# Embedding front in four groups with the mix on TensorE, parameter loads behind the row gathers, and three small reorderings behind the scan

## The chip, the cores and the metric

The kernel runs on one core of a Trainium2 chip. The core has five engines that run their own instruction lists side by side: TensorE (PE; its weight loads are PEld), VectorE (DVE), ScalarE (ACT), GpSimd (POOL) and SyncE (SP, used here to issue DMAs). They wait for each other on semaphores only. The metric is the device time of one execution in microseconds (us); the figure for a kernel is the median of its runs.

## What is computed

One layer of a small language model over 8 sequences of 256 tokens, 192 channels wide. Cut to what matters here:

```python
# embedding: 64 values of the token's row, and two mixes of 3 rows each
emb = emb_table[tokens]                                   # (8, 256, 64)
parts = [emb]
for i, spos in enumerate((spos0, spos1)):                 # spos: (3, 64)
    sel = softmax(emb[..., 3*i:3*(i+1)], axis=-1)
    parts.append(einsum('bsk,kd->bsd', sel, spos))
h = concatenate(parts, axis=-1) * sqrt(192) + positional_encoding(256, 192)

# selective-scan layer
n = layernorm(layernorm(h))                               # second with gamma, beta
xi, z = split(n @ W_in, 2)                                # 384 channels each
u = silu(depthwise_conv1d(xi))                            # 3 taps along the sequence
y = merge of a forward and a backward selective scan of u
h = h + (layernorm(y) * silu(z)) @ W_out + layernorm(h)

# mixture of experts, top 2 of 8
h = h + sum over the two experts picked by a router of gate * expert(layernorm(h))
```

## The kernel before, in words

**Tiles.** A tile (`t`) is 128 tokens on the 128 partitions; there are 16 (`TILES`). A group (`g`) is 4 tiles, 512 tokens, two sequences; there are 4 (`NG`). The 384 inner channels are 3 blocks (`blk`) of 128.

**Front, to about 88 us.** POOL gathers the token rows with 16 indirect DMAs, one per tile (L561), and only then builds `ident`, the unit matrix that every transpose on PE needs. Everything up to the second norm is done in two halves of 8 tiles (`HT`): `select` (L689 to L698) makes the softmax of the two triples with small DVE operations and one exponential on ACT (L1117); `mix_in` (L700) multiplies and adds the three `spos` rows over 8 tiles at a time, five DVE operations of 512 columns for each mix; of the second half, POOL does the second mix (L583, L586). `embed` (L711) scales, adds the position table and takes the moments; `norm_twice` (L719) applies both norms, with the roots from ACT (L1109, L1110) and one Newton step on DVE. The order on DVE is: the whole first half, `select(1)` and `mix_in(1, 0)`, `embed(1)`, `norm_twice(1)`, and only then `convolve(0)`. ACT scales the rows by the second root (`norm_in`, L1137, L1139), PE transposes them (`norm_transposes`), ACT applies gamma and beta (`keep_xn_t`, L1149), and PE multiplies with W_in (`in_products`, L1471 and L1474), two banks at a time for groups 2 and 3. DVE convolves from the banks (L776 to L780), ACT keeps z (L1160) and u (L1164). `keep_lb(0)` (L1171) opens the next stage, the time steps.

All 34 small parameter loads are on SP's queue in one list (L466) under one semaphore `s_par`. DVE, POOL, ACT and PE each wait for the whole list before the work that follows in their own lists.

**Scan, 140 to 614 us.** 192 turns, in each of which DVE scans, POOL multiplies, ACT makes decays and scaled inputs, and PE transposes. The change does not touch it.

**Behind the scan.** ACT issues the load of `w_out` after the last sum of PE (L1325). PE waits for it and for the last copy of y out of the banks (`s_yv`, written by DVE at L856) before `y_transposes(0)`. The router follows. Then DVE works out for each of the 39 slots of 128 rows (`SLOTS`) which rows it holds: `is_slot` (L1021, 32 x 39 = 1248 columns), its product with `row_hi` and with `row_lo` into `hot_a` (L1023, twice), the places `hot_b` in four parts (L1027), and PE multiplies the two (L1715) behind its `b2` products (L1709). From the result come `src_row` and `dst_row`.

**Slots, 694 to 880 us.** POOL gathers the 128 rows of a slot (L629), six or seven slots ahead; at first two gathers are issued and both are waited for (L634) before ACT hears of either. ACT copies the slot's rows (L1401) and weights (L1417), PE transposes (L1451), ACT keeps the transpose (L1409), PE multiplies (L1738, L1743, L1755), DVE squares the rectified sums, and POOL scatters the result.

## Time and profile before

| | us |
|---|---|
| median of 3 runs | 904.82 |
| lowest and highest run | 903.65 and 904.99 |
| the profiled execution, device time | 903.25 |
| its span, first to last instruction | 901.5 |

The device time of the profiled execution is 1.75 us more than its span. Busy shares over the whole span are PE 86%, PEld 78%, DVE 81%, ACT 72% and POOL 59%; the chain that ended last is PE for 47%, DVE for 22% and ACT for 17% of the span. These are means over stages with different limits, so the stages are read by themselves: the first 88 us, the 39 us behind the scan, the 41 us of routing, and the slots. In the rows, "idle before" is how long the engine stood still ahead of a group and the name behind the arrow is what ended that; PEclk is the granted TensorE clock as a share of 2.4 GHz.

### The profile page before, as it was taken

To read this page: it belongs to the slowest core of one execution; us is meant where nothing else is said; L and a number is where in the kernel's file an instruction comes from. 1 tells how busy PE (TensorE), PEld (TensorE's weight loads), DVE (VectorE), ACT (ScalarE), POOL (GpSimd) and SP (SyncE) were. 2 spreads that over 40 slices of the span, in tenths; PEclk is the share of its full clock that TensorE was granted. 3 is DMA by queue.
4 is the path that set the end of the run, shared out by engine and by line. 5 is a ranking of instruction groups with operands and counts; after the bars stand their busy time and mean duration, and the time that the engine had idled before them with its cause. 6 is when DMAs were issued, how large, how long until landed. Compare 5 with 4: busy or idle time off the path is not lost.

```text
span 901.5 us, 16654 instructions
## 1 busy us (share of the span) xinstructions
PE 778.9 (86%) x6060; PEld 706.4 (78%) x6061; DVE 730.8 (81%) x871; ACT 648.5 (72%) x1261; POOL 535.1 (59%) x343
## 2 busy tenths in 40 slices
PE   0389777899999999989999899996956999999990
PEld 0133336899998999989999899995855899999990
DVE  3788899789999899988999999998938455555554
ACT  0365999999999999989999999992331444444421
POOL 6430004799988999969999799892000444444420
PEclk9999988999999999999999999997955899999996
DMA  4003103355674754745746466376450111111106
GB/s 87 3 30 111 9 27 123 89 137 175 148 212 149 165 191 123 195 140 130 210 113 163 159 180 187 118 167 230 136 171 9 40 44 44 44 44 44 44 23 218
DMA packets 46453, 104.43 MB, mean 116 GB/s; under 512 B 16448, under 2 KB 25176, under 8 KB 46392
## 3 DMA queue, kind: packets, MB, share of 16 engines
q1 hardware_dynamic: 35784, 74.67, 25.6%
q0 software_dynamic: 8352, 27.07, 15.1%
q10 hardware_dynamic: 2256, 1.87, 0.6%
q8 instruction: 38, 0.62, 0.3%
q14 instruction: 23, 0.19, 0.1%
HBM read 83.77 MB, written 19.82 MB: 115 GB/s over the span
## 4 chain that ended last, share of the span: by engine, by line
PE 47%; DVE 22%; ACT 17%; POOL 7%; issue 4%; DMA 2%; DVEq 0%; ACTq 0%; POOLq 0%; SPq 0%
PE ps L1451 15%; PE ps L1755 8%; PE ps L1573 8%; DVE arena L851 8%; ACT arena L1278 6%; PE ps L1738 6%; POOL arena L625 5%; ACT arena L1261 4%; PE ps L1743 4%; ACT arena L1264 3%; PE ps L1471 2%; PE ps L1474 1%; DVE stats L672 1%; DVE arena L798 1%; PE ps L1673 1%
## 5 line engine op out<-in xcount | busy, mean ns | idle before, releaser
L625 POOL TENSOR_TENSOR arena<-arena 128x1024 f32<-128x1024 f32 x192 | 395.3, 2285 | 117.3 <-DVE arena L851 114.0
L851 DVE TENSOR_TENSOR_SCAN arena<-arena,ps 128x1024 f32<-128x1024 f32 x192 | 426.3, 2277 | 20.1 <-PE ps L1573 16.9
L1451 PE MATMUL ps<-ident,arena 128*128 128x128 f32 (+3 forms) x2622 | 349.3, 280 | 79.2 <-ACT arena L1139 37.7
L1451 PEld LDWEIGHTS ps<-ident,arena 128*128 128x128 f32 (+3 forms) x2622 | 299.7, 144 | 100.6 <-issue 52.0
L1278 ACT ACTIVATE arena<-arena,neg_a 128x510 f32<-128x510 f32 x384 | 241.0, 708 | 0.1
L629 POOL DMA_INDIRECT arena<-x_rows,arena x39 | 37.8, 970 | 160.2 <-DVE arena L1035 79.6
L1573 PE MATMUL ps<-arena,ln_in 128*128 128x128 f32 x768 | 104.0, 279 | 0.0
L1573 PE MATMUL ps<-arena 128*128 128x128 f32 x768 | 101.4, 275 | 0.0
L1573 PEld LDWEIGHTS ps<-arena,ln_in 128*128 128x128 f32 x768 | 96.0, 196 | 0.0
L1573 PEld LDWEIGHTS ps<-arena 128*128 128x128 f32 x768 | 93.3, 192 | 0.0
L1755 PE MATMUL ps<-arena,ln_in 128*128 x468 | 82.7, 327 | 0.8 <-DVE arena L1066 0.8
L1264 ACT ACTIVATE arena<-ident,arena 128x128 f32<-128x128 f32 x256 | 81.0, 388 | 0.0
L1755 PEld LDWEIGHTS ps<-arena,ln_in 128*128 128x128 f32 x468 | 75.1, 190 | 1.2 <-issue 1.1
L1261 ACT ACTIVATE arena<-ln_in,arena 128x384 f32<-128x384 f32 x128 | 68.1, 605 | 3.1 <-PE ps L1573 2.7
L1261 ACT ACTIVATE arena<-arena 128x384 f32<-128x384 f32 x128 | 67.9, 602 | 2.6 <-PE ps L1573 2.5
L637 POOL DMA_INDIRECT y_rows<-arena x39 | 38.5, 988 | 30.9 <-DVE arena L1066 19.1
L1409 ACT ACTIVATE arena<-ps 128x256 f32<-128x256 f32 x39 | 15.0, 384 | 56.2 <-PE ps L1451 56.2
L1053 DVE TENSOR_TENSOR ln_in<-ps,arena 128x384 f32<-128x384 f32 x40 | 22.1, 554 | 40.1 <-PE ps L1743 40.1
L1053 DVE TENSOR_TENSOR ln_in<-ps,ln_in 128x384 f32<-128x384 f32 x38 | 21.0, 553 | 34.3 <-PE ps L1743 34.3
L1417 ACT ACTIVATE arena<-arena 128x1158 f32 x20 | 23.4, 1170 | 33.4 <-issue 14.2
L1061 DVE SCALAR_TENSOR_TENSOR ln_in<-ln_in 128x384 f32<-128x384 f32 x78 | 43.5, 558 | 2.7
L1417 ACT ACTIVATE ln_in<-arena 128x1158 f32 x19 | 22.2, 1170 | 20.9 <-issue 17.4
(218 smaller groups left out, 882.5 us busy)
## 6 DMA issues: line engine op xcount, KB each, us to landing
arena<-b_rows SPq DMA_DIRECT2D x64, 512.0 KB, 4.0
arena<-ws SPq DMA_DIRECT2D x16, 576.0 KB, 6.3
arena<-wf POOLq DMA_DIRECT2D x16, 576.0 KB, 8.2
arena<-hf POOLq DMA_DIRECT2D x16, 576.0 KB, 7.9
summed_first<-arena SPq DMA_DIRECT2D x8, 576.0 KB, 5.4
summed_second<-arena SPq DMA_DIRECT2D x8, 576.0 KB, 7.3
arena<-summed_second SPq DMA_DIRECT2D x8, 576.0 KB, 5.8
gates_dram<-arena SPq DMA_DIRECT2D x4, 768.0 KB, 3.4
```

The costliest lines, as they stand in the source:

```text
L625: g_.tensor_tensor(state[i % STATES], state[i % STATES], c_bc[u % C_BUFS], ALU.mult).then_inc(s_mul, 1)
L851: v.tensor_tensor_scan(o, a, x, 0.0, ALU.mult, ALU.add).then_inc(s_scan, 1)
L1053: added = v.tensor_tensor(hid, ps[:, H_BANKS[half] + i, 0:HH].rearrange("p (a b) -> p a b", b=P), bias[:, 3 * i:3 * (i + 1)].unsqueeze(2). ...
L1061: v.scalar_tensor_tensor(hid, hid, 0.0, hid, ALU.max, ALU.mult).then_inc(s_h[i], 1)
L1261: a.activation(x_t[u % 2][:, t, :], dtu_t[g % 2][d][:, t, :], ACT.Copy, scale=bt[:, TG * g + t, col:col + 1])
L1264: last = a.activation(b_diag[u % 2][:, t, :], ident[:], ACT.Copy, scale=bt[:, TG * g + t, col:col + 1])
L1278: last = a.activation(out_a[:, n, :, lo:hi], src[:, :, lo:hi], ACT.Exp, scale=neg_a[:, blk, d, PAIR * pair + n:PAIR * pair + n + 1])
L1417: a.activation(w1_cur[half], w1_all[:, bass.ds(e * WC, WC)], ACT.Copy).then_inc(s_wc, 1)
L1451: return mm(o, src, ident[at:at + parts, at:at + parts], start=start, stop=True, is_transpose=True, skip_group_check=True)
L1573: last = mm(ps[:, bank + 1, P * t:P * t + P], dtu_t[g % 2][d][:, t, cols], b_diag[u % 2][:, t, :], start=True, stop=True)
L1738: mm(ps[:, H_BANKS[half] + j // 3, P * (j % 3):P * (j % 3) + P], w1_cur[half][:, P * j:P * j + P], slot_x_t[half][:, 0, :], start=j % 3 == ...
L1755: last = mm(ps[:, 3, 0:C], h_t[half][:, j, :], w2_all[:, bass.ds(e * (HB * C) + j * C, C)], start=j == 0, stop=j == HB - 1)
```

## The change

Front:

- POOL builds `ident` ahead of the gathers. The gathers count on four semaphores, one for each group.
- The select, the position sum and both norms go group by group, in an order written out by hand on DVE, ACT and PE in which the steps of several groups alternate.
- The mix becomes a product on PE: the six weights of each of a group's four tiles (24 columns) are transposed, ACT keeps the transpose, and one product of 24 rows with a block-diagonal `mix_w` (24 x 512, filled by eight small DMAs on ACT's queue) gives the 128 mixed values of all four tiles in one bank. DVE reads them from the bank.
- The position table is loaded twice over, so that it covers four tiles.
- SP's list is cut: the first 9 loads (channel constants, W_in, gamma and beta) count on `s_win`; the other 25 are issued once all rows have been gathered. The waits for `s_par` move behind the work that doesn't need it.
- The exponential of the decay rates and the waits for parameters move to later places; POOL's sum of residual and norm waits for groups instead of halves.

Behind the scan:

- PE's waits for `w_out` and for the router weights move from ahead of `y_transposes(0)` into the products that read them.
- `row_lo` depends on the partition only, so its product with `is_slot` becomes two ACT copies with a per-partition scale; PE waits for these too. `row_hi` is made directly.
- Slot 0 is gathered alone and ACT hears of it at once; then pairs (1, 2), (3, 4), (5, 6). ACT does `keep_x_t(0, 0)` before `copy_x(1, 1)`.

```diff
-            pool.wait_ge(s_tok, 16)   # ... 16 gathers, then ident
+            st.then(g_.memset(ident[:], 0.0))
+            g_.affine_select(out=ident[:], in_=ident[:], compare_op=ALU.not_equal, fill=1.0, base=0,
+                             pattern=[[-1, P]], channel_multiplier=1).then_inc(s_ident, 1)
+            pool.wait_ge(s_tok, 16)   # ... 16 gathers, .then_inc(s_rows[t // TG], 16)
...
-            for dst, src in loads:
+            for dst, src in loads[:WIN_LOADS]:
+                sp.dma_start(dst, src, allow_slow_non_contiguous=True).then_inc(s_win, 16)
+            for g in range(NG):
+                sp.wait_ge(s_rows[g], 16 * TG)
+            for dst, src in loads[WIN_LOADS:]:
                 sp.dma_start(dst, src, allow_slow_non_contiguous=True).then_inc(s_par, 16)
...
+            act.wait_ge(s_mix_z, 1)
+            for t in range(TG):
+                for i in range(2):
+                    row = SEL * t + NPOS * i
+                    act.dma_start(mix_w[row:row + NPOS, t, SUB * i:SUB * (i + 1)],
+                                  spos[:, NPOS * SUB * i:NPOS * SUB * (i + 1)].rearrange("o (k c) -> (o k) c", k=NPOS)).then_inc(s_mix_w, 16)
...
+            def select_transpose(g):
+                pe.wait_ge(s_sel_w, g + 1)
+                transpose(ps[0:TG * SEL, SEL_BANK, P * g:P * (g + 1)], sel_w[:, TG * g:TG * (g + 1)].rearrange("p t i k -> p (t i k)"), P).then_inc(s_sel_ps, 1)
+            def mix_product(g):
+                if g == 0:
+                    pe.wait_ge(s_mix_w, 16 * 2 * TG)
+                pe.wait_ge(s_sel_t, g + 1)
+                if g == 3:
+                    pe.wait_ge(s_emb, 1)
+                mm(ps[:, MIX_BANKS[g], :], sel_t[g % 2], mix_w.rearrange("p t c -> p (t c)"), start=True, stop=True).then_inc(s_mix_ps, 1)
...
# DVE, front order
-            select(0); mix_in(0, 0); mix_in(0, 1); embed(0); norm_twice(0)
-            select(1); mix_in(1, 0); embed(1); norm_twice(1)
+            select_logits(0); embed_rows(0); select(0); embed_mix(0)
+            select_logits(1); embed_rows(1); norm_first(0); select(1); norm_rows(0); norm_second(0)
+            select_logits(2); embed_rows(2); select(2); embed_mix(1)
+            select_logits(3); embed_rows(3); norm_first(1); select(3); norm_rows(1); norm_second(1)
+            embed_mix(2); embed_mix(3); norm_first(2); norm_rows(2); norm_second(2)
+            norm_first(3); norm_rows(3); norm_second(3)
+            dve.wait_ge(s_win, 16 * WIN_LOADS)
...
# ACT, front order
+            select_exp(0); keep_sel_t(0); first_root(0); select_exp(1); second_root(0); keep_sel_t(1); norm_in(0)
+            select_exp(2); keep_sel_t(2); act.wait_ge(s_win, 16 * WIN_LOADS); keep_xn_t(0)
+            first_root(1); select_exp(3); second_root(1); keep_sel_t(3); norm_in(1)
+            first_root(2); first_root(3); second_root(2); keep_xn_t(1); norm_in(2); second_root(3)
+            # then neg_a, and keep_z(0, blk)
...
# PE, front order
+            select_transpose(0); mix_product(0); select_transpose(1); mix_product(1)
             norm_transposes(0)
+            select_transpose(2); mix_product(2); pe.wait_ge(s_win, 16 * WIN_LOADS)
             pe.wait_ge(s_xn_t, 2)
             in_products(0, (0, 1))
+            select_transpose(3); mix_product(3)
             in_products(0, (2,))
             norm_transposes(1)
+            pe.wait_ge(s_emb, 3)
             in_products(0, (3, 4))
+            pe.wait_ge(s_emb, 4)
             in_products(0, (5,))
...
             pe.wait_ge(s_yv, NG)
-            pe.wait_ge(s_w_out, 16)
-            pe.wait_ge(s_wr, 1)
             def out_product(g):
+                pe.wait_ge(s_w_out, 16)
...
-            for h, part in enumerate((row_hi, row_lo)):
-                st(v.tensor_tensor(hot_a[:, :, h, :], is_slot, each(part[:], SLOTS), ALU.mult))
+            v.tensor_tensor(hot_a[:, :, 0, :], is_slot, each(row_hi[:], SLOTS), ALU.mult).then_inc(s_hot_a, 1)
+            # on ACT:
+            for k in range(TOP):
+                rows_k = slice(TILES * k, TILES * (k + 1))
+                a.activation(hot_a[:, rows_k, 1, :], is_slot[:, rows_k, :], ACT.Copy, scale=row_lo[:, k:k + 1]).then_inc(s_hot_a, 1)
...
-            for s in range(0, AHEAD, 2):
+            gather(0)
+            gathered(1, 1)
+            for s in range(1, AHEAD, 2):
                 gather(s)
                 gather(s + 1)
                 gathered(s + 2, 2)
-            gather(AHEAD)
```

## Rows read from the trace of the kernel before

**Rows 1.** Engine busy times by stage: routing, and slots; PEclk, DMA share, GB/s last.
```profile
653.00:694.00 41.00, 29.08 (x148) 26.14 (x148) 25.55 (x120) 9.44 (x17) 0.00 (x0) 0.54 0.30 100
705.00:876.00 171.00, 170.78 (x1436) 161.63 (x1437) 94.77 (x190) 71.92 (x147) 69.42 (x71) 1.00 0.15 42
```

**Rows 2.** Timeline of POOL, front: start, us, engine, line, operation, idle before.
```profile
2.80 1.10 POOL L561 DMA_INDIRECT arena<-emb,tok_sb  x1 [2.28 <-DMA tok_sb<-tok]
...
20.91 1.15 POOL L561 DMA_INDIRECT arena<-emb,tok_sb  x1 [0.30 <-issue]
22.37 1.14 POOL L561 DMA_INDIRECT arena<-emb,tok_sb  x1 [0.30 <-issue]
...
23.96 1.40 POOL L566 TENSOR_SCALAR_AFFINE_SELECT ident<-ident 128x128 f32<-128x128 f32 x1 [0.23 <-issue]
```

**Rows 3.** POOL's DMA queue: packets, MB, share, in 2 to 9.5 and 2 to 25 us.
```profile
q0 software_dynamic: 128, 0.13, 8.6%
...
q0 software_dynamic: 512, 0.53, 12.0%
```

**Rows 4.** Timeline of DVE, front.
```profile
15.96 0.21 DVE L696 TENSOR_TENSOR arena<-arena 128x48 f32<-128x48 f32 x1
16.20 0.69 DVE L706 TENSOR_TENSOR ln_in<-arena 128x512 f32<-128x512 f32 x1
...
23.45 1.76 DVE L715 SCALAR_TENSOR_TENSOR resid<-ln_in,arena 128x1536 f32<-128x1536 f32 x1
25.25 2.18 DVE L672 BATCH_NORM_STATS2 stats<-resid 128x6 f32<-128x192 f32 x8
...
29.81 2.40 DVE L729 TENSOR_SCALAR ln_in<-resid,mv,rs 128x192 f32<-128x192 f32 x8
...
38.53 1.43 DVE L706 TENSOR_TENSOR arena<-arena 128x512 f32<-128x512 f32 x1
```

**Rows 5.** Timeline of ACT, front.
```profile
33.10 1.49 ACT L1137 ACTIVATE arena<-ln_in,rs 128x192 f32<-128x192 f32 x4 [2.47 <-DVEq L734]
...
88.18 0.76 ACT L1171 ACTIVATE arena<-ps,row_one,row_scale 128x512 f32<-128x512 f32 x1
```

**Rows 6.** Timeline of PE, front.
```profile
35.19 1.94 PE L1451 MATMUL ps<-ident,arena 128*128 128x128 f32 x8 [35.19 <-ACT arena L1139]
38.92 3.38 PE L1471 MATMUL ps<-arena 128*128 128x512 f32 x4 [1.79 <-ACT arena L1149]
...
58.94 1.97 PE L1451 MATMUL ps<-ident,arena 128*128 128x128 f32 x8 [2.47 <-ACT arena L1139]
...
67.39 1.88 PE L1471 MATMUL ps<-arena 128*128 128x512 f32 x4
```

**Rows 7.** Timeline of SP's queue, front: the last of the 34 loads.
```profile
20.52 0.72 SPq L466 DMA_DIRECT2D b_sb<-b  x1
```

**Rows 8.** Timeline behind the scan, DVE and PE.
```profile
616.81 1.75 DVE L856 COPY arena<-ps 128x1536 f32<-128x1536 f32 x1
...
620.63 2.79 PE L1451 MATMUL ps<-ident,arena 128*128 128x128 f32 x12 [4.93 <-DMA arena<-w_out]
```

**Rows 9.** Timeline of the slot tables, PE and DVE.
```profile
681.21 8.44 PE L1709 MATMUL ps<-b_sb,ln_in 8*128 8x192 f32 x32 [0.68 <-ACT ln_in L1392]
...
685.99 1.45 DVE L1023 TENSOR_TENSOR arena<-arena,row_lo 128x1248 bf16<-128x1248 f32 x1
...
692.16 0.70 PE L1715 MATMUL ps<-arena 128*128 128x78 bf16 x8 [0.44 <-DVE arena L1027]
```

**Rows 10.** Timeline of the first slots, POOL, ACT, PE.
```profile
694.14 1.09 POOL L629 DMA_INDIRECT arena<-x_rows,arena  x1 [79.59 <-DVE arena L1035]
...
698.24 0.36 ACT L1401 ACTIVATE arena<-arena 128x192 f32<-128x192 f32 x1 [1.90 <-POOLq L634]
...
698.95 0.94 POOL L629 DMA_INDIRECT arena<-x_rows,arena  x1 [2.44 <-DMA arena<-x_rows,arena]
...
705.22 1.57 PE L1738 MATMUL ps<-arena,ln_in 128*128 128x128 f32 x12 [0.52 <-issue]
```

More of the change, by code:

```diff
@@ L213, in build @@
         sel_r = cut([TILES, 2])
-        mix = [cut([HT, SUB]) for _ in range(2)]
+        mix_w = cut([TG, 2 * SUB], parts=TG * SEL)
+        sel_t = [cut([P], parts=TG * SEL) for _ in range(2)]
         used[0] = after_params
@@ L396, in build @@
         s_place = sem("places_ready")
+        s_is_slot = sem("slot_flags_ready")
+        s_hot_a = sem("row_parts_ready")
         s_held = sem("held_product")
@@ L650, in _ @@
                 pool.wait_ge(s_y, s + 2)
+                if s and s + AHEAD - 1 < SLOTS:
+                    gathered(s + AHEAD, 1)
                 if s + AHEAD < SLOTS:
-                    gathered(s + AHEAD + 1, 1)
-                if s + AHEAD + 1 < SLOTS:
-                    gather(s + AHEAD + 1)
+                    gather(s + AHEAD)
                 scatter(s)
@@ L661, in _ @@
             st = Steps(dve, v_step)
+            v.memset(mix_w, 0.0).then_inc(s_mix_z, 1)
             v.memset(w_x, 0.0)
@@ L700, in mix_in @@
-            def mix_in(h, i):
-                half = slice(HT * h, HT * (h + 1))
-                dst = ln_in[:, half, SUB * (i + 1):SUB * (i + 2)]
-                for k in range(NPOS):
-                    o = dst if k == 0 else mix[0]
-                    st.then(v.tensor_tensor(o, spos_sb[:, i:i + 1, k, :].to_broadcast([P, HT, SUB]),
-                                            sel_w[:, half, i, k:k + 1].to_broadcast([P, HT, SUB]), ALU.mult))
-                    if k:
-                        st.then(v.tensor_tensor(dst, dst, mix[0], ALU.add))
@@ L721, in norm_twice, with of_group @@
-            def norm_twice(h):
-                half = slice(HT * h, HT * (h + 1))
-                dve.wait_ge(s_rstd, h + 1)
-                newton(HT * h, HT, mv, rs)
-                st.then(v.tensor_tensor(nt1[:, half], rs[:, half], rs[:, half], ALU.mult))
-                v.tensor_tensor(mv2[:, half, 1], mv[:, half, 1], nt1[:, half], ALU.mult).then_inc(s_ln_in, 1)
-                for t in range(HT * h, HT * (h + 1)):
+            def of_group(g):
+                return slice(TG * g, TG * (g + 1))
@@ new lines, in embed_mix, with norm_first @@
+            def embed_mix(g):
+                dve.wait_ge(s_mix_ps, g + 1)
+                embedded(g, slice(SUB, C), ps[:, MIX_BANKS[g], :].rearrange("p (t c) -> p t c", t=TG)).then_inc(s_emb, 1)
+                dve.wait_ge(s_emb, g + 1)
+                st.wait()
+                moments(lambda t: resid[:, TG * g + t, :], TG * g, TG, mv, s_ln)
+            def norm_first(g):
+                group = of_group(g)
+                dve.wait_ge(s_rstd, g + 1)
+                newton(TG * g, TG, mv, rs)
+                st.then(v.tensor_tensor(nt1[:, group], rs[:, group], rs[:, group], ALU.mult))
+                v.tensor_tensor(mv2[:, group, 1], mv[:, group, 1], nt1[:, group], ALU.mult).then_inc(s_ln_in, 1)
@@ L781, in convolve @@
                                            cv[:, :, 0:SEQ - 1], ALU.mult, ALU.add).then_inc(s_conv, 1)
-            norm_twice(1)
+            select_logits(0)
+            embed_rows(0)
+            select(0)
+            embed_mix(0)
+            select_logits(1)
+            embed_rows(1)
+            norm_first(0)
+            select(1)
+            norm_rows(0)
+            norm_second(0)
+            select_logits(2)
+            embed_rows(2)
+            select(2)
+            embed_mix(1)
+            select_logits(3)
+            embed_rows(3)
+            norm_first(1)
+            select(3)
+            norm_rows(1)
+            norm_second(1)
+            embed_mix(2)
+            embed_mix(3)
+            norm_first(2)
+            norm_rows(2)
+            norm_second(2)
+            norm_first(3)
+            norm_rows(3)
+            norm_second(3)
+            dve.wait_ge(s_win, 16 * WIN_LOADS)
             convolve(0)
             convolve(1)
+            dve.wait_ge(s_par, 16 * PAR_LOADS)
             constants()
```

196 lines of the change are left out of this document (99 added, 97 removed).

## Prediction

> **What bounds the kernel now.** I read the stages first, since the busy shares of the whole are a mean over them. The slots run at PE's own pace: PE is busy 170.78 of 171 us at the full clock [rows 1], and the change leaves the 39 slots' work alone. The scan is 192 equal turns that the change leaves alone too. So what can move is the start of the scan, the stretch between scan and slots, and the first slot. Then the timelines of one engine after another, front first, with the question who ends each engine's idle time.
>
> In the front, PE has its first work at 35.19 us and its first product with W_in at 38.92 [rows 6]. Before that it is a chain of DVE: the first eight tiles are gathered, DVE mixes them with ten operations of 512 columns at 0.69 us [rows 4], scales and adds (1.76), takes moments, norms, and ACT gets the first rows at 33.10 [rows 5]. PE then works on group 0 and 1 and stands still again for 2.47 us until the second half has been normed (58.94, [rows 6]). From 67.39 it runs six pairs of blocks without a gap, and the stage ends where ACT opens the time steps, 88.18 [rows 5]. The front is bound by its serial chain, not by any engine's work: the lever is when the first rows reach PE, and that each later group is ready when PE asks.
>
> Behind the scan PE stands still 4.93 us, and what ends it is the load of w_out [rows 8]. In the routing DVE makes tables while PE waits, at a mean granted clock of 0.54 [rows 1]; the first slot waits until 698.24 for two gathers, though it needs one [rows 10].
>
> **The front, step by step.** The new order has three engines handing work around, so I lay it out from the rows and carry one clock time along. Handoffs cost 0.05 us each.
>
> *Rows arrive.* POOL's queue has moved 128 packets of its 512 by 9.5 us, a quarter, so the first four gathers have landed by then; all 512 by 25 [rows 3]. `ident` first costs POOL nothing: memset and select (1.40) fit into the 2.28 us for which it waits for the tokens [rows 2]. What hides it is that load; without it, it would cost some 1.9. I take 9.6, 14.6, 19.7 and 25.2 for the groups. ACT's eight small loads are issued long before 9.6 (ACT has nothing else until then); they land in time unless each took over 1 us.
>
> *Group 0 to PE.* Two select operations on DVE 0.4 and rows to place 0.35 (256 of the 1536 columns of the 1.76 us operation, plus start), exponential on ACT hidden behind the latter, three small operations 0.6 (0.21 each, [rows 4]): weights at 11.0. PE transposes 24 columns. No row shows this shape; the nearest are eight full transposes in 1.94 [rows 6], so 0.25 to 0.7, taken 0.45. ACT's copy 0.3. The product of 24 rows with 512 columns: a full 128-row one takes 3.38 / 2 = 1.7 on the same slow clock and about half that later [rows 6]; the depth is smaller but not the columns, so I take 1.75 (0.85 to 2.5). DVE reads the bank 0.8, moments 1.5 (half of 2.18 plus aggregation): 16.0. DVE then does the logits and rows of group 1 (0.75), six operations of 0.2 for the first norm (as the 0.21 of [rows 4]), the weights of group 1 (0.6), four rows of norm at 0.30 (2.40 / 8), four operations more (0.83): 20.6. The root on ACT (two small operations, 0.5) hides behind group 1's work. ACT's `norm_in(0)` is one half of what it did, 1.9: 22.6. It began at 33.10; now at 20.65.
>
> *First product.* PE transposes 1.94: 24.6; then, ahead of the product in PE's list, the weights of group 2 (0.45), ACT's copy 0.3 and the 1.38 for gamma and beta, the mix product 1.75 beside it: W_in starts at 27.2 instead of 38.92. That is **11.7 us**.
>
> *Holding it.* PE: first pair 4.4, then group 3's weights, copy and mix 2.6, third block 2.1, transposes 1.0, pair 2.8, last block 2.1: 42.2. Group 3's rows (25.2) are asked for at 25.8, so there is 0.6 us of slack. Next late is ACT's copy of z behind `norm_in(2)` and the last root: ACT is busy from 39.8, hands over at 43.6, so PE stands still 1.4. From there PE's list has no gap: 3.0 + 2.1 + 1.0 + 2.8 + 2.1 + 1.0 reaches group 2's products at 55.7, before at 67.4 [rows 6]. DVE's convolutions begin at 43.1, behind the last norm, at 2.3 a block, and keep ahead of PE by 0 to 2 us. Six pairs follow, and the stage ends at 76.4 instead of 88.18: **11.8 us**.
>
> *What else moves.* The 25 late loads: SP issued its 34 from 2.4 to 20.52 + 0.72 = 21.24 [rows 7], 0.55 us apiece, so 25 of them take from 25 to 39, landed by 42. First reader is the projection at 73 on PE and the constants on DVE at 59, so 17 us of cover; SP's next duty, storing the gates, comes at about 54. POOL's sums start at 44 and are wanted after 90. The second mix leaves POOL; beside it DVE's multiplications had taken 1.43 instead of 0.69 [rows 4], and that cost is gone too (it is in the 11.8).
>
> The Trainium skill ("SBUF — State Buffer", section "Who interferes with whom") says that a DVE operation with two SBUF inputs and a GpSimd one that reads SBUF block each other; the 1.43 beside 0.69 agrees. The same section speaks against the new order: single-input DVE operations in a two-port mode keep GpSimd from writing the descriptors of its gathers. The norm rows and copies now run while gathers are issued. What the rows show of that: the last two gathers start 1.46 us apart, once DVE's wide operations run; if the last four have that pitch, the first eleven steps had (20.91 - 3 x 1.45 - 2.80) / 11 = 1.25 [rows 2]. At 1.45 for the eight others too the last group lands 1.6 later, 1.0 more than its slack: at most 1 us of the 11.8.
>
> **Behind the scan.** `y_transposes(0)` still needs the banks free: DVE's copy ends at 616.81 + 1.75 = 618.56 [rows 8]. So it starts at 618.6, not 620.63: **2.0 us**, all of it passed on, since ACT and DVE stand idle for its result. w_out is next read by `out_product(0)` some 8 us later and has landed by 620.6. Between 1 and 2.
>
> **Slot tables.** DVE loses one operation of 1.45 [rows 9]; ACT, idle, does two halves in about 0.7 each, beside DVE's product with `row_hi`. The parts of `hot_b` come 1.45 earlier, but PE is in its b2 products until 681.21 + 8.44 = 689.65 [rows 9] and then has 32 products of some 0.07: 691.85 instead of 692.86. **1.0 us** (0.5 to 1.45).
>
> **First slots.** The gather of slot 0 starts at 694.14 and alone should land in 2.7; ACT can copy at 696.9, not 698.24, and PE gets the first product 1.3 earlier. But gather 1 is now issued only behind it, after the 0.7 us that POOL takes from landing to the next gather (ACT hears at 698.24, POOL starts the next at 698.95, [rows 10]), and slots 1 and 2 land at 701.5. ACT's copies then queue: x of slot 1, its weights (1.17), x of slot 2, and the second slot's products start at 704.35 instead of 705.22 [rows 10]. **0.9 us** (0 to 1.4). Also 3.41 us of DVE sums gate the first transpose at 697.5, no later than the new order asks.
>
> **Sum:** 11.8 + 2.0 + 1.0 + 0.9 = 15.7. Span 901.5 - 15.7 = 885.8, device time of the profiled execution 903.25 - 15.7 = 887.6; against the median of 904.8 it gives 889.1. The forecast is 888.5, between the two.
>
> **Rivals.** *The front gives less.* Three handoffs (DVE, PE, ACT, PE, DVE) take the place of DVE's private mix. At 0.1 a handoff it is 0.9 dearer, with products at 2.5 another 2.2, with late gathers 1: the front gives 8 and the time is 892.3. For it: PE at the start is at half clock. Against: slack in DVE's own list.
>
> *The front gives more.* If PE has the full clock by its first products, mixes cost 0.85 and the layout ends 1.6 earlier; if the routing, shifted against the clock's changes, gets the full clock for some of its 41 us (now 0.54, [rows 1]), 2 to 3 more: 884.5.
>
> *The tail pieces don't do what they say.* The waits for the y copy, for DVE's last sums and for slot 1's gather take the place of those removed; 2 us go: 890.5. For it: each of the three has a second wait within 2 us.
>
> *Slower.* The scan is not changed but is entered with its engines in another phase. DVE's scan and POOL's product run side by side there, and [rows 4] show what DVE can lose beside a reading POOL (1.43 for 0.69). If the new phase makes the two overlap more, so that each of the 192 turns is 0.1 us longer, 19.2 us are lost against 15.7 won and it is 908. It decides from (15.7 + 1.8) / 192 = 0.09 us a turn on. Against: everything that feeds the first turn shifts together, and turns are long compared with the handoffs.
>
> **How the numbers follow.** As laid out 0.60; front gives less 0.20; front gives more 0.12; tail pieces void 0.05; slower scan 0.03. The range 884.0 to 893.5 takes in the first four with their bounds. About 0.2%, 1.8 us, is what a measurement of this kernel can tell from no change; within it would need the front to give nothing, which no row supports: 0.01, taken out of the second case. Faster 0.96, slower 0.03.
>
> **What would show it.** ACT's first scaling of rows at 20 to 22 us; first W_in product at 26 to 29; no PE gap over 2 us from there; the opening of the time steps at 75 to 79; the first transpose behind the scan waiting for DVE's copy and not for w_out; PE's last table product within 0.3 of the end of its b2 products plus 2.3; PE busy all through the slots as before. Wrong would be a W_in product after 31, a row group landing after 27, or a scan whose 192 turns take over 2 us longer in all.

## The result, and the profile after

The changed kernel takes 889.45 us (888.67 to 890.06, 4 runs) against 904.24 (903.4 to 904.99) for the kernel before on the same chip: a ratio of 0.9836, 95% interval 0.9819 to 0.9853. The forecast was 888.5 in 884.0 to 893.5. The profiled execution after has 889.05 us and a span of 887.3, against 903.25 and 901.5.

In words, the stages of both profiled executions, each from one event to the next:

| stretch | before | after | gain |
|---|---|---|---|
| start to ACT's opening of the time steps | 88.18 | 76.30 | 11.88 |
| to DVE's first turn of the scan | 56.09 | 56.97 | -0.88 |
| to DVE's last copy of y | 472.54 | 473.39 | -0.85 |
| to PE's `b2` products | 64.40 | 61.86 | 2.54 |
| to POOL's first slot gather | 12.93 | 11.81 | 1.12 |
| to PE's second slot of products | 11.08 | 10.41 | 0.67 |
| to the end | 196.28 | 196.56 | -0.28 |
| span | 901.5 | 887.3 | 14.2 |

So two stretches that the change does not touch, the time steps and the scan, give back 1.73 us of what was won, and the slots another 0.28. That is the part that the prediction did not have, and many of the experiments below are about it.

The front first. Timeline of the kernel after, POOL, DVE, ACT and PE (start, us, engine, line, operation, idle before and what ended it); the rows answer to [rows 2, 4 to 6]:

```profile
1.25 0.28 POOL L571 TENSOR_SCALAR_AFFINE_SELECT ident<-ident 128x128 f32<-128x128 f32 x1 [0.24 <-POOL ident L570]
2.77 1.12 POOL L575 DMA_INDIRECT arena<-emb,tok_sb  x1 [1.24 <-DMA tok_sb<-tok]
...
20.43 0.94 POOL L575 DMA_INDIRECT arena<-emb,tok_sb  x1 [0.30 <-issue]
21.68 0.94 POOL L575 DMA_INDIRECT arena<-emb,tok_sb  x1 [0.30 <-issue]
...
10.47 0.18 DVE L695 TENSOR_REDUCE arena<-arena 128x8 f32<-128x24 f32 x1 [7.62 <-DMA arena<-emb,tok_sb]
...
14.95 0.69 DVE L689 SCALAR_TENSOR_TENSOR resid<-ps,arena 128x512 f32<-128x512 f32 x1 [3.04 <-PE ps L1513]
...
21.66 1.49 ACT L1163 ACTIVATE arena<-ln_in,rs 128x192 f32<-128x192 f32 x4 [1.39 <-DVEq L735]
...
12.06 0.37 PE L1497 MATMUL ps<-ident,arena 128*24 128x128 f32 x1 [12.06 <-DVE arena L708]
12.88 2.04 PE L1513 MATMUL ps<-arena 24*128 24x512 f32 x2 [0.45 <-ACT arena L1147]
...
28.19 3.78 PE L1530 MATMUL ps<-arena 128*128 128x512 f32 x4
...
43.62 1.96 PE L1530 MATMUL ps<-arena 128*128 128x512 f32 x4 [0.55 <-ACT arena L1180]
...
55.51 1.88 PE L1530 MATMUL ps<-arena 128*128 128x512 f32 x4
```

To see: PE's first work is a transpose at 12.06, not at 35.19; W_in's first product comes at 28.19, not at 38.92; and the only idle time of PE from there on is 0.55 us. The unit matrix took 0.28 us at 1.25, where before it took 1.40 at 23.96, beside DVE's two-input operation that ran from 23.45 to 25.21 [rows 2, 4]; behind the first (1.12) every gather takes 0.94 or 0.95, and from the second on each starts 1.25 behind the one before it, to the end, where the last ones had taken 1.15 and 1.14.

Behind the scan, timeline of PE, DVE, ACT and POOL after; they answer to [rows 8 to 10]:

```profile
608.46 1.93 PE L1497 MATMUL ps<-ident,arena 128*128 128x128 f32 x12 [2.92 <-DVE arena L874]
...
671.85 1.52 ACT L1439 ACTIVATE arena<-arena,row_lo 128x624 bf16<-128x624 f32 x2 [3.38 <-DVE arena L1039]
...
676.80 2.26 PE L1785 MATMUL ps<-arena 128*128 128x78 bf16 x32
...
680.33 1.10 POOL L625 DMA_INDIRECT arena<-x_rows,arena  x1 [75.93 <-DVE arena L1052]
...
683.34 0.36 ACT L1447 ACTIVATE arena<-arena 128x192 f32<-128x192 f32 x1 [0.51 <-POOLq L630]
...
688.07 0.36 ACT L1447 ACTIVATE arena<-arena 128x192 f32<-128x192 f32 x1 [3.06 <-POOLq L630]
```

The first transpose behind the scan now waits for DVE's copy and no longer for w_out; the 32 table products run in one piece straight behind the `b2` products; ACT copies slot 0's rows 3.01 us after the gather is issued, where it had taken 4.10 (698.24 - 694.14).

What was lost lies in the granted clock (1.00 is the level of 2.4 GHz, 0.50 that of 1.2 GHz). The first two rows are windows of the kernel before, in the time steps and behind the start of a scan group (the scan goes through the four groups one after another); the next three are windows of the kernel after, over a product in the time steps and behind two such starts. Columns: window, length, busy time of PE, PEld, DVE, ACT, POOL, then PEclk, DMA share, GB/s:

```profile
108.00:116.00 8.00, 5.52 (x10) 2.57 (x11) 7.86 (x6) 7.33 (x10) 0.00 (x0) 0.79 0.03 8
...
276.40:286.20 9.80, 9.80 (x91) 9.74 (x91) 9.49 (x5) 9.50 (x21) 8.98 (x6) 1.00 0.29 112
```

```profile
98.60:104.06 5.46, 5.46 (x7) 2.36 (x8) 5.36 (x4) 3.71 (x4) 0.00 (x0) 0.50 0.01 3
...
265.00:275.00 10.00, 10.00 (x79) 10.00 (x78) 8.79 (x5) 8.56 (x18) 8.00 (x5) 0.84 0.38 126
...
500.40:510.00 9.60, 9.60 (x75) 9.60 (x74) 8.50 (x5) 7.75 (x16) 7.62 (x5) 0.83 0.30 100
```

At each start of a scan group PE is idle for over a third of some 9.7 us, and behind that the clock either stays at 1.00 (before, 276 us: 91 products in 9.80 us) or falls for a while (after, 265 us: 79 in 10.00, 0.84). Such a fall is called a dip below. From one of DVE's copies of y to the next there were 117.11, 118.72 and 114.34 us before, and 118.72, 117.10 and 115.77 after: a dip costs 1.4 to 1.6 us. Before has one at these three starts, after has two; with the stretch ahead of the first start 0.57 shorter (121.80 for 122.37) that is the 0.85.

### The profile page after: what moved, and what is told of

It is laid out like the page before. It is cut to its first block, busy times and chain, and to the rows that moved or that the text cites. A ratio compares the mean times of both kernels' runs of the same rounds, so it can differ in the third digit from the quotient of the medians.

```text
span 887.3 us, 16729 instructions
## 1 busy us (share of the span) xinstructions
PE 786.0 (89%) x6072; PEld 707.1 (80%) x6073; DVE 721.1 (81%) x890; ACT 651.6 (73%) x1275; POOL 525.6 (59%) x339
## 4 chain that ended last, share of the span: by engine, by line
PE 51%; DVE 20%; ACT 17%; POOL 5%; issue 4%; DMA 2%; ACTq 0%; DVEq 0%; POOLq 0%; SPq 0%
PE ps L1497 16%; DVE arena L869 9%; PE ps L1825 8%; PE ps L1643 8%; ACT arena L1319 6%; PE ps L1808 6%; ACT arena L1302 4%; POOL arena L621 4%; PE ps L1813 4%; ACT arena L1305 2%; PE ps L1530 2%; PE ps L1533 1%; PE ps L1742 1%; DVE stats L670 1%; ACT arena L1327 1%
```

## Experiments

The kernels ran in three groups, with the kernel before beside each, at 905.48, 905.14 and 904.86 us. Stages are read in each one's profiled execution.

### One half of the change alone

`front_only` is the changed kernel with the work behind the scan as before (the `row_lo` product in two halves on DVE); `tail_only` the kernel before with the three pieces behind the scan. The core of the edit that tells them apart:

```diff
# front_only, from the changed kernel
+            pe.wait_ge(s_w_out, 16)
+            pe.wait_ge(s_wr, 1)
             def y_transposes(g):
...
+            for k in range(TOP):   # row_lo part on DVE again
...
-AHEAD = 7
+AHEAD = 6
```

> The front of the changed kernel with the parts behind the scan as before. Theory (the pieces add): the time steps open at 76.3 us as in the changed kernel, not 88.2, and some 1.7 us of the 11.9 are given back between there and the end of the scan, as in the changed kernel, because TensorE's granted clock rises at other moments after its idle gaps; nothing is won behind the scan. Time 10.2 us under the kernel before, 894.0. Rival A (the 1.7 us are given back by something that the new front leaves behind, such as the late parameter loads on SP's queue): same time here, but then the kernel whose parameter loads are early gets them back. Rival B (the pieces behind the scan depend on the new front): more than 14 us are missing from the sum of this kernel and the one with the tail alone.

> The kernel before with only the parts behind the scan changed: w_out wait moved, low row part on ScalarE, slot 0 gathered alone with AHEAD 7. Theory: time steps open at 88.2, and from there to the end of the scan it takes 528.6 us as before; then 2.0 us at the w_out wait, 0.5 in the routing, 1.1 at the row parts and 0.7 at the first slots: 4.3 us under the kernel before, 899.9. Rival (the tail pieces are covered by second waits and what was seen came from shifted clock phases): within 1.5 us of the kernel before, 902.7 or more.

`front_only` took 892.53 us, ratio 0.9866 (0.9848 to 0.9884): 12.1 us for the front. `tail_only` took 901.36, ratio 0.9958 (0.9941 to 0.9974): 3.8 us for the three pieces, where 3.9 was forecast. These gains are worked out from the ratios; the medians lie 12.95 and 4.12 apart. Together 15.9 against the 14.8 measured for both; each gain is known to about 1.6 us only, which leaves room for a plain sum. The rival that the tail pieces win under 1.5 us is out (the interval is 2.3 to 5.3). `front_only` did better than its forecast of 10.2: its time steps open at 75.08 and not at 76.3, and only the scan gave something back. In `tail_only` the time steps took 56.10 and the scan 472.63, in `front_only` 56.08 and 473.23.

### Where the front's gain sits: the unit matrix, and the place of the mix

`ident_late` builds the unit matrix behind the 16 gathers again. `mix_dve` keeps the four groups, the early unit matrix and the new orders, and does the mix with DVE operations of 256 columns.

```diff
# ident_late
-            st.then(g_.memset(ident[:], 0.0))
-            g_.affine_select(out=ident[:], in_=ident[:], ...).then_inc(s_ident, 1)
             pool.wait_ge(s_tok, 16)   # ... 16 gathers
+            st.then(g_.memset(ident[:], 0.0))
+            g_.affine_select(out=ident[:], in_=ident[:], ...).then_inc(s_ident, 1)
# mix_dve, DVE
-                dve.wait_ge(s_mix_ps, g + 1)
-                embedded(g, slice(SUB, C), ps[:, MIX_BANKS[g], :].rearrange("p (t c) -> p t c", t=TG)).then_inc(s_emb, 1)
+                for i in range(2):
+                    for k in range(NPOS):
+                        o = mix_t if k else dst
+                        st.then(v.tensor_tensor(o, spos_sb[...], sel_w[...], ALU.mult))
+                        if k:
+                            st.then(v.tensor_tensor(dst, dst, mix_t, ALU.add))
+                embedded(g, slice(SUB, C), mixed).then_inc(s_emb, 1)
```

> The changed kernel with the unit matrix built behind the 16 gathers, as in the kernel before. It is ready at about 23.2 us. Theory (the mix on TensorE hangs on it, and the front's chain has no slack from there): the first transpose of weights starts at 23.3 instead of 12.1, the first product with W_in at 39 to 40 instead of 28.2, the time steps open at 87 to 89, so the whole gain of the front is gone: 900 to 901. Rival (only the first group is late, and since all rows are in by then the later groups catch up): the time steps open at 79 to 82 and the time is 892 to 895.

> The changed kernel with the mix done by VectorE in four groups (ten operations of 256 columns a group, position rows loaded by broadcast as before) and no transposes of weights or mix products; all else, the order of the groups too, as changed. Theory (the mix on TensorE is what pays: DVE is the front's next bound): ten operations of 0.39 us replace a handoff of 3.0 us, so group 0 is 1 us later at ACT (about 22.6), the first W_in product is at 28 as in the changed kernel, but DVE has 15.6 us more work with under 6 us of idle time to put it in, so the convolutions start some 10 us later (54 instead of 43.9), and the time steps open at 86 to 88. Time 899 to 901. Rival (the split into groups is what pays, since it lets PE begin early): the time steps open at 77 to 80 and the time is 890 to 893.

`ident_late` took 901.82 us, ratio 0.9948 (0.9931 to 0.9965): as `tail_only`, so the front's gain is gone. Its time steps open at 87.22, against 88.18 before. Timeline of its PE:

```profile
23.37 0.39 PE L1497 MATMUL ps<-ident,arena 128*24 128x128 f32 x1 [23.37 <-POOL ident L576]
24.20 2.04 PE L1513 MATMUL ps<-arena 24*128 24x512 f32 x2 [0.45 <-ACT arena L1147]
```

The transpose of the weights waits for `ident` until 23.37, 11.31 us later than after, and W_in's first product is at 39.43, 11.24 later. Once the mix is on PE, the unit matrix is the head of the front's chain; before, PE had no use for it until 35.19.

`mix_dve` took 908.24 us, ratio 1.0037 (1.0022 to 1.0051): slower than before, though it has all of the front but the mix on PE, and all of the tail. Its first W_in product comes early (31.84), but the time steps open at 95.60. Groups of instructions of its DVE, 9 to 95 us (line, operation, operands, count, busy us and mean ns, idle before), and its window from the first W_in product to the opening:

```profile
L719 DVE TENSOR_TENSOR arena<-arena 128x256 f32<-128x256 f32 x24 | 10.2, 426 | 0.9 <-DVE rs L683 0.2
L775 DVE TENSOR_SCALAR arena<-ps,chan_sb 128x512 f32<-128x512 f32 x12 | 9.7, 804 | 5.8 <-PE ps L1512 5.6 <-DVE rs L683 0.2
...
L722 DVE TENSOR_TENSOR arena<-arena 128x256 f32<-128x256 f32 x16 | 6.8, 425 | 0.5
```

```profile
31.84:95.60 63.76, 52.99 (x129) 18.64 (x129) 53.82 (x145) 29.52 (x65) 6.83 (x2) 0.84 0.14 49
```

The mix is 40 operations and 17.0 us of DVE, which also has to convolve before PE's banks come free. PE is busy 52.99 of 63.76 us there, at a granted clock of 0.84; in the kernel after it is busy 47.21 of 48.11, at 1.00. PE's four stops in this window (3.25, 1.67, 1.95 and 3.89 us) are ended by DVE or by ACT, which had itself waited 15.3 us for DVE's moments; the stage lost these stops and the longer products at the lower clock. The opening was forecast at 86 to 88, so the loss is right in kind and some 8 us larger than thought. The other kernels of its group, with the mix on PE, opened at 79.97 to 80.38. So four groups without the move to PE don't pay in this order of operations, which was written for a mix on PE; an order made for DVE was not tried.

### Whether the late loads cost the time steps

`par_early` issues the 25 late loads at once, with no wait for the rows.

```diff
-            for g in range(NG):
-                sp.wait_ge(s_rows[g], 16 * TG)
             for dst, src in loads[WIN_LOADS:]:
```

> The changed kernel, but SP issues the 25 late parameter loads right behind the 9 early ones, without waiting for the row gathers. Theory (the loads are small and in nobody's way): gathers keep their pitch of 1.25 us, DVE's first operation on rows starts within 0.5 us of the 10.47 of the changed kernel, the time steps open at 76.3 within 0.5, and the time is that of the changed kernel, 889.5 within 1.0. Rival A (their thousands of 4-byte packets hold up the gathers): DVE's first operation at 12 or later and each group 1 to 3 us later, time 891 to 893. Rival B (late loads cost something after the front): time steps plus scan are back at 528.6 instead of 530.4 us, time 887.7.

It took 889.27 us, ratio 0.9825 (0.9799 to 0.9851), no different from the changed kernel within some 2.4 us. W_in at 28.24, time steps open at 75.67; these steps took 56.09 and its scan 473.44. So the cut of SP's list neither buys nor costs anything that can be measured, and it isn't what lengthens the scan.

### The pieces behind the scan, one by one

```diff
# wout_wait_back
             pe.wait_ge(s_yv, NG)
+            pe.wait_ge(s_w_out, 16)
+            pe.wait_ge(s_wr, 1)
# rowlo_dve: DVE again, 2 operations of 624 columns
-                a.activation(hot_a[:, rows_k, 1, :], is_slot[:, rows_k, :], ACT.Copy, scale=row_lo[:, k:k + 1]).then_inc(s_hot_a, 1)
+                v.tensor_tensor(hot_a[:, rows_k, 1, :], is_slot[:, rows_k, :], row_lo[...], ALU.mult).then_inc(s_hot_a, 1)
# weights_first
-            copy_x(1, 1)
             copy_w(1, 1)
+            copy_x(1, 1)
```

> The changed kernel with PE's waits for w_out and the router weights back ahead of the first transposes behind the scan. Theory: the gap of TensorE there grows from 2.9 to 4.9 us and is ended by the DMA; 2.0 us are lost down to the first slot: 891.4. Rival (ACT's and DVE's own work sets the start of the second transposes anyway): under 0.7 us lost, 890.1 or less.

> The changed kernel with the low row part made on VectorE by two products of 624 columns in place of ACT's two copies. Theory: DVE takes 1.5 us more ahead of the places, but TensorE is busy with the b2 products for 0.4 of that, so the last table product ends 1.1 us later: 890.5. Rival (the end of the b2 products sets it alone): no difference, 889.5.

> The changed kernel, but ACT copies the second slot's weights before it waits for that slot's rows. In the changed kernel ACT stands idle 3.06 us for those rows, then copies rows and weights (1.17 us), and TensorE waits 1.45 us for it. Theory (ACT's order is what ate part of the gain of gathering slot 0 alone): the wait shrinks to 0.3 to 0.6 us and the time is 1.0 us less: 888.5. Rival (the gather of slots 1 and 2 itself sets the second slot): under 0.3 us.

The totals (896.32, 893.79 and 894.94 us; ratios 0.9898, 0.9877 and 0.9884) can't be set against 889.45: all kernels of this group had a front that was 4 us later, of which below. Their stages can.

*The wait for w_out.* From DVE's last copy of y to the `b2` products: 63.91 us with the wait put back, 61.77 to 62.01 in the six other kernels of the first two groups that have the new order. The price is 2.0 us, so its rival (under 0.7) is out. Timeline of `wout_wait_back`, PE:

```profile
613.19 1.09 PE L1497 MATMUL ps<-ident,arena 128*128 128x128 f32 x4 [4.87 <-DMA arena<-w_out]
```

*The row parts.* From the end of the `b2` products to the first slot gather: 4.49 us before (12.93 - 8.44), 4.45 in `rowlo_dve` (12.64 - 8.19), 3.47 in the changed kernel. The two ACT copies are worth 1.0 us. But in `front_only`, which has the parts on DVE as well, it is 3.47 too (14.07 - 10.60): there the `b2` products took 10.60 us instead of the 8.2 to 8.9 of most kernels, and DVE was done behind them. This window of `wout_wait_back`, which had the same 10.60, shows why:

```profile
673.33:683.93 10.60, 10.60 (x34) 10.16 (x35) 8.93 (x15) 1.52 (x2) 0.00 (x0) 0.50 0.00 0
```

At 0.50 from end to end, 32 products take 10.60; after has 8.34 at 0.64.

*Weights ahead of rows.* The second slot's products start 5.61 us behind the first, as in most others. That says little on the order of ACT's copies: PE ran this slot at the lower clock, its twelve products took 2.90 instead of the 1.57 of the kernel after, and it had no wait for ACT in front of the second slot ([0.52 <-issue], 694.87). Inconclusive.

### The same kernel again, and the clock filled by hand

`after_again` is the changed kernel, unaltered. `clock_steps` puts 26 transposes of the unit matrix into a free bank in PE's 3.29 us of idle time in the time steps; `clock_slots` puts 10 behind the table products, ahead of slot 0; `clock_all` has both, and the early loads.

```diff
# clock_steps
+                            if g == 2 and d == 0 and blk == 0:
+                                for _ in range(26):
+                                    transpose(ps[:, 0, 0:P], ident[:], P)
                             pe.wait_ge(s_pl, 2 * (g - 1) + d + 1)
# clock_slots
             last.then_inc(s_held, 1)
+            pe.wait_ge(s_passed, 2)
+            for _ in range(10):
+                transpose(ps[:, 0, 0:P], ident[:], P)
             pe.wait_ge(s_acc, 1)
```

> The changed kernel once more, on the chip that also runs the next three kernels. In the group of experiments before this one all kernels with the new front had the W_in product at 31.8 to 32.8 us, where the changed kernel had it at 28.19; the 4 us lay between VectorE's small norm operations in the first norm of group 0, with no semaphore behind them. If this comes from the chip or the execution, the three kernels of this group and this one show the same W_in time, all near 28.2 or all near 32.4. If it comes from the kernel's code, this one is at 28.2 whatever the chip. Time 889.5 (887 to 892) with the early front, 893.5 (892 to 896) with the late one; ratio to the kernel before 0.9836 or 0.988. Time-steps stage 56.08 or 56.97, nothing between.

> The changed kernel with 26 transposes of the identity into a free PSUM bank in the 3.29 us in which TensorE is idle in the time-steps stage. Theory (the 0.88 us that this stage lost is TensorE's clock after the gap, not the late loads): the product behind the gap takes 4.3 us or less instead of 5.46, the stage from the opening to the scan's first turn takes 56.1 or less, in this run and whenever it is profiled, and the total falls by 0.9 against a run of the changed kernel whose stage was 56.97, and by 0 against one whose stage was 56.08. Rival (the late loads or bank order cost it): the stage stays at 56.97. Second rival (the dummy work itself delays the product by running into its start): stage 57.5 or more.

> The changed kernel with 10 transposes of the identity into a free PSUM bank after the last table product, in the 4.84 us in which TensorE waits for the first gathered rows. Theory (slots 0 and 1 run at half the clock because TensorE idled before them: first slot to second 5.59 us against 4.53 later): first product to second slot's product 4.6 to 5.0 us and the first slot's product 2.6 us at most, total 1.0 to 2.0 us below the changed kernel of the same chip. Rival A (the clock falls all the same, the dummies stop too early or are too few): 5.6 us and the total as the changed kernel, within 0.5. Rival B (the first slots are held by the weight conversion of ScalarE, not by TensorE): product times fall but the second slot starts no earlier, total within 0.5.

> Both of the clock edits, and the parameter loads no longer held behind the row gathers. If the gains add: 0.9 from the time steps where the changed kernel's stage was 56.97, 1 to 2 from the slots, and 0 to 0.3 from the loads, so 886.5 to 888 with the early front (W_in at 28.2), 890.5 to 892 with the late one. If the loads, issued at once, take bandwidth from the gathers, the W_in product comes over 0.5 us later than in the other kernels of this chip; a single look has it at 28.24 against 28.19, so no such cost is expected.

Measured: 894.15, 891.76, 892.89 and 896.59 us; ratios 0.9881 (0.9864 to 0.9899), 0.9882 (0.9856 to 0.9908), 0.9875 (0.9857 to 0.9892) and 0.9903 (0.9884 to 0.9922).

*The unaltered kernel* has time steps of 56.09 us and a scan of 472.66, the values of before (56.09, 472.54), and one dip among its three group starts (117.10, 118.73, 114.35). So the new code does not force either loss. Over all 14 profiles the steps take 56.08 to 56.10 or 56.97 to 56.98 and nothing between. Four of the twelve kernels with a new front have the long value (the changed kernel, `ident_late`, `mix_dve`, `weights_first`), and neither of the two with the old one (the kernel before and `tail_only`). The scan takes 472.3 to 472.7 in these two, in `after_again` and in `clock_all`, and 473.2 to 474.1 in the other ten. Whether the new front makes the long values likelier is not shown; two profiles of the old one are too few to tell.

*The steps.* The product behind the 3.29 us gap, in the kernel before, in the kernel after, in `after_again` and in `clock_steps` with the gap filled (timeline of PE):

```profile
110.48 4.29 PE L1543 MATMUL ps<-arena 128*128 128x512 f32 x6 [3.29 <-DVE arena L807]
```

```profile
98.60 5.46 PE L1613 MATMUL ps<-arena 128*128 128x512 f32 x6 [3.29 <-DVE arena L825]
```

```profile
101.53 4.34 PE L1613 MATMUL ps<-arena 128*128 128x512 f32 x6 [3.29 <-DVE arena L825]
```

```profile
98.88 3.06 PE L1497 MATMUL ps<-ident 128*128 128x128 f32 x26
102.00 2.84 PE L1616 MATMUL ps<-arena 128*128 128x512 f32 x6
```

The granted clock over the last three is 0.50, 0.65 and 1.00, and their stage 56.97, 56.09 and 56.09. Over the 14 profiles it goes together without exception: where this product takes 5.45 or 5.46 the stage is long (four), where it takes 2.81 to 4.51 it is short (ten). So the clock behind the gap is the cause of the 0.88, as the expectation had it. `clock_steps` alone would not show it, since three kernels with the gap left open have 2.81 as well. The edit buys nothing where the stage is short already. That another engine sets the stage there fits DVE's load (busy 48.29 of 49.97 us from 83.30 on in the kernel after), but was not tested. Its ratio, equal to that of `after_again`, says the same.

*The slots.* In `clock_slots` slot 0's products took 1.58 us at a granted clock of 1.00, in all other kernels 2.90. But `clock_all` has the same ten transposes in the same place, and stayed at 0.50 (timelines of PE, `clock_slots` and then `clock_all`):

```profile
687.24 1.58 PE L1813 MATMUL ps<-arena 128*128 128x128 f32 x12 [0.56 <-ACT arena L1457]
```

```profile
690.80 2.90 PE L1814 MATMUL ps<-arena 128*128 128x128 f32 x12 [0.56 <-ACT arena L1455]
```

So the filling raised the clock in one profile of two. Where it did, the second slot started 5.49 behind the first instead of 5.62: the faster products did not bring the second slot forward, and its rival B, ACT's work, fits what the timeline of ACT in `clock_slots` shows:

```profile
690.05 0.36 ACT L1449 ACTIVATE arena<-arena 128x192 f32<-128x192 f32 x1 [2.96 <-POOLq L630]
...
690.79 1.17 ACT L1465 ACTIVATE ln_in<-arena 128x1158 f32 x1 [0.23 <-issue]
...
691.87 0.35 ACT L1449 ACTIVATE arena<-arena 128x192 f32<-128x192 f32 x1
...
692.26 0.36 ACT L1457 ACTIVATE arena<-ps 128x256 f32<-128x256 f32 x1
```

ACT hears of slot 1's rows at 690.05, which is the landing of the gather, and copies these rows, slot 1's weights (1.17 us) and the rows of slot 2 before it keeps the transpose that PE waits for. PE stands still 0.93 and 1.67 us meanwhile, falls back in its clock (0.81 over its next twelve products) and takes 6.15 us for the next slot, as in `after_again` (6.18), where the kernel after took 4.60. The filling won at slot 0 what it could not keep at slot 1.

*No version beats the changed kernel.* `clock_all` has the shortest scan of all (472.30) and is last of its group: its W_in product is at 33.56, its `b2` products took 10.60 and its first two slots 12.32 us, where after has 10.19. It was forecast at 890.5 to 892 for a late front, so that forecast failed. The test that it set for the early loads, W_in over 0.5 us later than in the others of its group, came out positive (33.56 against 30.40 to 32.23). The gathers were hardly held up, though: behind the first all but one kept their pitch of 1.25 us and DVE's first operation on rows came at 10.20; what came late is DVE, of which next.

### A front that is 2 to 5 us later in two of three groups

Where the unit matrix is made early, W_in's product came at 27.7 to 28.2 us in the first measurement and the first group. In the second and third group it came at 30.4 to 33.6, in all eight kernels, the unaltered one (30.4) among them. Timeline of DVE after, and of `clock_steps`, in the same steps, whose code is the same:

```profile
20.81 0.16 DVE L679 TENSOR_TENSOR nt<-rs 128x4 f32<-128x4 f32 x1
21.01 0.16 DVE L680 SCALAR_TENSOR_TENSOR nt<-mv,nt 128x4 f32<-128x4 f32 x1
21.21 0.17 DVE L681 TENSOR_SCALAR nt<-nt 128x4 f32<-128x4 f32 x1
```

```profile
23.15 0.17 DVE L679 TENSOR_TENSOR nt<-rs 128x4 f32<-128x4 f32 x1 [2.41 <-remote]
23.86 0.16 DVE L680 SCALAR_TENSOR_TENSOR nt<-mv,nt 128x4 f32<-128x4 f32 x1 [0.55 <-DVE nt L679]
25.25 0.17 DVE L681 TENSOR_SCALAR nt<-nt 128x4 f32<-128x4 f32 x1 [1.23 <-DVE nt L680]
```

Nothing that the profile shows was outstanding: the one operand that is not DVE's own, ACT's root `rs`, was finished by 19.50 in `clock_steps`, the operations last as long as ever, and the time is between them. The first gap is put down to `remote`, which names no engine. The gaps come to 2.0 us in all (`mix_dve`) to 5.7 (`clock_all`), the longest single one to 3.73 (`rowlo_dve`). It is not the code (`after_again`), nor the chip (the first and the third group ran on the same one), nor the late loads (`par_early` and `clock_all` both have them early, with W_in at 28.24 and 33.56). The Trainium skill ("Runtime: NRT & Kernel Launch", section "Instruction fetch mechanics") says that each engine refills its instructions in blocks by a DMA of its own and that this is mostly hidden. The trace has such a queue, but its one packet of these microseconds lies at 24 to 26 in the kernel after and at 28 to 30 in `clock_steps`, moved with the delay rather than ahead of it; so a slow refill is neither shown nor excluded. The cause stays open, and whether taking the profile has a part in it was not tested. The kernel before shows nothing of it in its times (904.24 to 905.48). So the measured gain of the change is 14.8 us in the first measurement and 10.7 in the third group (904.86 - 894.15). The profiled execution of that group's unaltered kernel (891.67) has gaps of 3.3 us in all and opens the time steps 2.92 us later than the kernel after; the stages of its slower executions are not known.

## Why the prediction was right, point by point

**The chain.** Right in kind and nearly in every time. The rows were heard of at 10.47 and not at 9.6, the weights were ready at 11.9 instead of 11.0, the mix product took 2.04 instead of 1.75 (inside the stated 0.85 to 2.5), ACT's first scaling came at 21.66 instead of 20.65 and W_in at 28.19 instead of 27.2: one microsecond late throughout, most of which (0.87) the landing of the rows had put in at the start. The handoffs took 0.03 to 0.15 us instead of 0.05; the transpose, at 0.37, was cheaper than 0.45. The microsecond came back at the next stop: PE's idle time behind group 0 was 0.55, not 1.4, and from 43.6 the layout holds to 0.2 (group 2's products at 55.51 against 55.7, the opening at 76.30 against 76.4). So 11.88 for 11.8; the error of 1.0 had slack below it.

**The unit matrix.** "Costs POOL nothing" was right (0.28 us ahead of the tokens). That without it the front would gain next to nothing was not said; `ident_late` showed W_in 11.24 later and the opening 10.92 later.

**Gathers and DVE.** The worry that norms and copies on DVE would slow the gathers, worth up to 1 us, did not come true: beside DVE's L728 (19.44 to 20.77) and the L689 at 22.02 the gathers kept 0.94 and 1.25. By the Trainium skill ("SBUF — State Buffer", section "Who interferes with whom") single-input operations such as L728 can block POOL if they run in a two-port mode; no row here shows it. The other half of that section, that two SBUF inputs of DVE contend with a GpSimd operation that reads SBUF, agrees with the select, which took 1.40 beside such an operation and 0.28 without. Gathers, too, took 1.14 to 1.15 from 18.02 on in the kernel before, with two-input operations of 512 columns running, and 0.94 ahead of them.

**w_out.** 2.0 us forecast; the stretch gained 2.54, of which the wait is 2.0 (`wout_wait_back`). The rest, 0.5, is in the routing, where `front_only` has as much (0.7) without any edit there; what it comes from was not tested.

**Slot tables.** 1.0 forecast, 1.0 shown (4.49 to 3.47), with the reason given: PE is in its `b2` products until then. The condition that goes with it was missing: at half the clock these take 10.60, and in `front_only`, where they did, the parts on DVE cost nothing.

**First slots.** 0.9 forecast, 0.67 measured. ACT copied slot 0's rows 3.01 us after the issue of its gather instead of 2.76, and heard of slot 1's rows after 7.74 instead of 7.4. From there to the second slot's products it took 2.67 where 2.85 was forecast (704.35 - 701.5), so ACT's list was laid out rightly, and what was taken too low is the landing of the rows.

**What the sum lacked.** 15.7 forecast, 14.2 measured in the span. The stretches laid out gave 16.2; the time steps and the scan gave back 1.73 and the slots 0.28. The prediction named a clock that shifts with the stages, but only on the gaining side; the loss is the same mechanism with the other sign. The rival of a slower scan had another one (POOL beside DVE, 0.09 us a turn): the 192 turns are 0.85 longer in all, 0.004 each, and `after_again` has none of it.

**The range, and luck.** Right for the recorded measurement, 1 us from the forecast. Part of that nearness is luck: the stretches laid out gave 0.5 more than forecast and the clock took 1.7, and neither was foreseen. The unaltered kernel in the third group, 894.15, is outside the range by 0.65: the gaps in DVE's list at 20 us were not among the cases.

## What to carry to other kernels

When work moves to an engine, look for what that engine needs that nobody else did: here a unit matrix that takes 0.28 us decided over some 11 us. A serial chain at the start is worth cutting in small groups only if the engine in the middle of it is relieved too. And before a loss of a microsecond in an untouched stage is explained by the change, profile the same kernel twice: five places here (the steps, the starts of scan groups, the `b2` products, the second slot, DVE at 20 us) took different values under the same instructions, 0.9 to 5 us apart.

## What was not expected of the hardware

- The clock behind a short idle time is not fixed. Behind the same 3.29 us of PE idle time, with the same work in front, six products took 5.46 us (0.50), 4.34 (0.65) or 2.81 (1.00, `clock_slots`).
- At the starts of scan groups PE is idle for about 3.6 of 9.8 us; the clock falls behind it in some and stays in others of the same execution, and this costs 1.4 to 1.6 us of a group of 114 to 119.
- From 9 to 28 us the granted clock of the kernel after reads 1.00, and yet the mix product took 2.04 us there and 1.12 at 33.93, W_in's four products 3.78 and 1.88 at 38.02. The products tell the clock better than the column does there.
- DVE stood still for up to 3.73 us at a time between small operations, with nothing outstanding that the profile shows, in eight profiles and not in four others with the same instructions there or nearly so.
